# Where and when the tokens of attention and MLP are turned in the fused third stage

## What is computed

```python
x = x + _L0_attn_ref(_layernorm(x), Wkqv, bkqv, Wp, bp)      # causal attention, 16 heads
x = x + _L0_ffn_ref(_layernorm(x), gate_w, ...)              # 16 experts, top 4, and a shared one
x = x + _L1_attn_ref(_layernorm(x), wq, wk, wv, wo)          # 16 heads of 8, hyperbolic distance
x = x + _L1_ffn_ref(_layernorm(x), w1, b1, w2, b2)           # relu(x @ w1 + b1) @ w2 + b2
```

## Time and profile before

| what | us |
|---|---|
| median of 3 runs | 2449.32 |
| lowest, highest | 2448.59, 2451.76 |
| profiled execution, its time | 2456.33 |
| profiled execution, its span | 2454.2 |
| third stage's loop in it, end of the first `dve_ratio` of body 0 to that of body 31 | 1343.48 to 2372.66 |

### The profile page before, as it was taken

The page is one execution under the profiler, slowest core; times in us unless marked ns, Lnnn a source line. Parts: engine busy times, 40 slices in busy tenths (PEclk is TensorE's granted clock), DMA queues, the critical chain, the costliest instruction groups (busy, mean ns, idle before and its releaser), DMA issues. The chain is left out here.

```text
span 2454.2 us, 50808 instructions
## 1 busy us (share of the span) xinstructions
PE 2089.9 (85%) x15438; PEld 1566.8 (64%) x15438; DVE 1956.8 (80%) x5939; ACT 1767.4 (72%) x3085; POOL 1627.2 (66%) x1866
## 2 busy tenths in 40 slices
PE   4999999999999996999997677777777778777876
PEld 4677777777777775888885445555555555555554
DVE  4677776776777774778775899999999999999992
ACT  2666666666666762444432799999999999999996
POOL 2776676766666750000001899999999999999993
PEclk7999999999999996999997579888888988889888
DMA  5000000000000003353450466776666777666674
GB/s 142 1 2 2 2 1 2 2 1 2 1 2 1 2 2 70 86 119 76 96 114 10 93 127 130 139 138 128 124 119 127 141 141 134 119 129 124 129 142 80
DMA packets 81388, 184.24 MB, mean 75 GB/s; under 512 B 9479, under 2 KB 31530, under 8 KB 81195
## 3 DMA queue, kind: packets, MB, share of 16 engines
q0 software_dynamic: 36864, 134.23, 29.1%
q1 hardware_dynamic: 36010, 43.38, 7.9%
q10 hardware_dynamic: 8320, 4.19, 0.7%
HBM read 42.85 MB, written 4.72 MB: 19 GB/s over the span
## 5 line engine op out<-in xcount | busy, mean ns | idle before, releaser
L1557 POOL TENSOR_TENSOR spare<-spare,u 128x1024 f32<-128x1024 f32 x192 | 456.2, 2376 | 16.0
L542 ACT ACTIVATE prob<-s_ps,nmax 128x128 f32<-128x128 f32 (+1 forms) x1024 | 364.4, 432 | 132.2 <-DVE nmax L599 132.2
L599 DVE CUSTOM_DVE_ANT_0 s_ps<-s_ps,mask 128x128 f32<-128x128 f32 (+1 forms) x1024 | 340.7, 385 | 100.7 <-issue 76.4
L1633 DVE TENSOR_SCALAR u<-d_ps 128x1024 f32<-128x1024 f32 x256 | 312.1, 1219 | 48.7 <-PE i_ps L1374 48.1
L579 POOL TENSOR_TENSOR g_lo<-g_all,g_hi 128x512 fp32r<-128x512 f32 x256 | 329.1, 1286 | 21.4
L1637 DVE SCALAR_TENSOR_TENSOR u<-i_ps,u 128x1024 f32<-128x1024 f32 x256 | 313.5, 1225 | 13.2 <-DVE u L1633 0.5
L1374 PE MATMUL d_ps<-rowsT 28*128 28x256 f32 x1024 | 144.7, 357 | 149.5 <-DVE u L1637 145.9
L534 ACT COPY g_all<-g_ps 128x512 f32<-128x512 f32 x256 | 151.5, 592 | 162.6 <-PE g_ps L63 161.5
L1514 ACT ACTIVATE u<-u 128x1024 f32<-128x1024 f32 x256 | 257.0, 1056 | 1.7 <-DMA u<-spare 1.6
L1517 ACT ACTIVATE u<-u 128x1024 f32<-128x1024 f32 x256 | 255.7, 1051 | 0.0
L1374 PEld LDWEIGHTS d_ps<-rowsT 28*128 28x128 f32 x1024 | 92.4, 208 | 246.3 <-issue 241.7
(11 more groups left out here) (275 smaller groups left out, 5795.2 us busy)
## 6 DMA issues: line engine op xcount, KB each, us to landing
u<-spare POOLq DMA_DIRECT2D x256, 512.0 KB, 12.2
w_all<-w_rows SPq DMA_DIRECT2D x128, 256.0 KB, 5.9
x<-L_attn_x ACTq DMA_DIRECT2D x8, 512.0 KB, 13.9
y<-x SPq DMA_DIRECT2D x32, 128.0 KB, 10.0
wkqv<-L_attn_Wkqv SPq DMA_DIRECT2D x4, 528.0 KB, 8.9
gate_rows<-L_ffn_gate_proj SPq DMA_DIRECT2D x1, 512.0 KB, 14.4
up_rows<-L_ffn_up_proj SPq DMA_DIRECT2D x1, 512.0 KB, 11.1
down_cols<-L_ffn_down_proj SPq DMA_DIRECT2D x1, 512.0 KB, 13.0
```

What stands on the lines that cost most here:

```text
L542: last = nc.scalar.activation(prob[:, kind, at, :].rearrange("p c n -> p (c n)"), s_ps[kind][:, at.start * P:at.stop * P], ACT.Exp, bias=n ...
L599: last = nc.vector.tensor_tensor_reduce(out=scores, in0=scores, in1=keep.mask[:, N - width:N], scale=-1.0, scalar=3.4e38, op0=ALU.add, op1 ...
L1557: nc.gpsimd.tensor_tensor(extra, extra, pair, ALU.mult).then_inc(prod_done, 1)
L1633: nc.vector.tensor_scalar(u[:, slot(i, p), :], d_ps[:, :], 0.0, None, ALU.max).then_inc(dist_done, 1)
```

## The change

The two pairs of transposes leave step 0 of PE's body and the bank `misc`. They go to the end of step 7 of the body before, behind the projection and the last transposes of rows, into `o_ps` (all 512 columns), whose content DVE has copied out by then (`o_copied`). ACT's one copy reads `o_ps` instead of `misc`. `pe_turn_x4` thereby takes batch b-3 in body b in place of b-4 in body b, so it stands one body earlier in the list than before, by a few instructions. The round of `pe_keep_busy` in step 7, which wrote into `o_ps`, is removed. Since `pe_y` writes `o_ps` too, PE now waits in step 0 for ACT's copy (`xT_done`, in the last body `late_xT4_done`) before `pe_y`. The wait for `res_done` moves from the transposes to `pe_qkv`. In the prologue PE waits for ACT's copy of w1 (`w1_folded`) and turns batch 1 before the loop; the wait for `w1_folded` in `pe_hidden` is dropped.

```diff
--- before.py
+++ after.py
@@ -1251,7 +1251,7 @@
     VALUES_AT = (2, 3, 4, 5)
     BACK_AT, ATTN_AT, PROJECT_AT = 4, 6, 7
     HIDDEN_AT = (1, 3)
-    BUSY_AHEAD, BUSY_BEHIND = {5: 1}, {4: 4, 7: 1}
+    BUSY_AHEAD, BUSY_BEHIND = {5: 1}, {4: 4}
     HW = WB // 2
     NORM_BEHIND, NORM4_BEHIND = 2, 5
     with ExitStack() as stack:
@@ -1336,15 +1336,15 @@
 
         def pe_turn_x(pe, b):
             pe.wait_ge(xh_done, (b + 1) * TB)
-            after(pe, res_done, b - 3)
-            after(pe, hi_done, b * TB)
-            after(pe, qkv_taken, b * TB)
+            after(pe, xT_done, b)
             for j in range(TB):
-                last = nc.tensor.transpose(misc[:, j * P:(j + 1) * P], xh[:, j, :], keep.ident)
+                last = nc.tensor.transpose(o_ps[:, j * P:(j + 1) * P], xh[:, j, :], keep.ident)
             last.then_inc(xh_turned, 1)
 
         def pe_qkv(pe, b, j):
             pe.wait_ge(xT_done, b + 1)
+            if j == 0:
+                after(pe, res_done, b - 3)
             after(pe, hi_done, b * TB + j)
             after(pe, qkv_taken, b * TB + j)
             nc.tensor.matmul(misc[:, 0:3 * P], xTs[:, 0, j * P:(j + 1) * P], keep.qkvoT[:, 0:3, :], start=True,
@@ -1423,6 +1423,7 @@
 
         def pe_fold_w1(pe):
             pe.wait_ge(weights_in, 16 * 5)
+            pe.wait_ge(xT_done, 1)
             nc.tensor.matmul(o_ps[:, :], zsum[:, :], w1_rows[:, :], start=True, stop=False)
             nc.tensor.matmul(o_ps[:, :], last_row[:, :], b1_row[:, :], start=False, stop=True).then_inc(w1_ready, 1)
 
@@ -1433,8 +1434,6 @@
             last.then_inc(x4_turned, 1)
 
         def pe_hidden(pe, b, half, rows_read):
-            if half == 0:
-                pe.wait_ge(w1_folded, 1)
             pe.wait_ge(rowsT_done[half], rows_read)
             after(pe, relu_done, 2 * b - 1 + half)
             for n in range(HW):
@@ -1465,14 +1464,14 @@
         def act_xT(act, b):
             act.wait_ge(xh_turned, b + 1)
             after(act, qkv_ready, b * TB)
-            nc.scalar.copy(xTs[:, 0, :], misc[:, 0:N]).then_inc(xT_done, 1)
+            nc.scalar.copy(xTs[:, 0, :], o_ps[:, 0:N]).then_inc(xT_done, 1)
 
         def act_both_xT(act, b, b4):
             act.wait_ge(xh_turned, b + 1)
             act.wait_ge(x4_turned, b4 + 1)
             after(act, qkv_ready, b * TB)
             after(act, h_ready, 2 * b4)
-            nc.scalar.copy(xTs[:, :, :].rearrange("p s n -> p (s n)"), misc[:, :]).then_inc(xT_done, 1)
+            nc.scalar.copy(xTs[:, :, :].rearrange("p s n -> p (s n)"), o_ps[:, :]).then_inc(xT_done, 1)
 
         def act_hi(act, b, j):
             act.wait_ge(qkv_ready, b * TB + j + 1)
@@ -1712,18 +1711,14 @@
                     pe_turn_rows(pe, 0, p)
                 pe_pairs(pe, 0, 0, 0)
                 pe_fold_w1(pe)
+                pe.wait_ge(w1_folded, 1)
+                pe_turn_x(pe, 1)
 
                 def body(b, i, one_before, two_before, three_before, four_before, five_before, one_after, two_after):
                     for p in range(HP):
                         following = next_pair(b, p, one_after)
                         if following:
                             pe_pairs(pe, *following, i if p + 1 < HP else (i + 1) % TURN)
-                        if one_after and p == 0:
-                            pe_turn_x(pe, b + 1)
-                        if four_before and p == 0:
-                            if not one_after:
-                                pe.wait_ge(res_done, b - 2)
-                            pe_turn_x4(pe, b - 4, (i - 4) % TURN, misc, N)
                         if one_after and p == 1:
                             pe_qkv(pe, b + 1, 0)
                         for r in {0: (5, 6), 1: (7,)}.get(p, ()):
@@ -1748,15 +1743,22 @@
                         if one_after:
                             for r in {6: (2,), 7: (4,)}.get(p, ()):
                                 pe_turn_rows(pe, b + 1, r)
+                        if p == HP - 1 and one_after:
+                            if one_before:
+                                pe.wait_ge(o_copied, 2 * b)
+                            if two_after:
+                                pe_turn_x(pe, b + 2)
+                            if three_before:
+                                pe_turn_x4(pe, b - 3, i, o_ps, N)
                         if one_before:
-                            if p == HP - 1:
-                                pe.wait_ge(o_copied, 2 * b)
                             pe_keep_busy(BUSY_BEHIND.get(p, 0))
+                        if p == 0 and one_after:
+                            pe.wait_ge(xT_done, b + 2)
+                        if p == 0 and not one_after:
+                            pe.wait_ge(late_xT4_done, 1)
                         if five_before and p == 0:
                             pe_y(pe, b - 5, 2 * (b - 1))
                         if four_before and p == HIDDEN_AT[0]:
-                            if not one_after:
-                                pe.wait_ge(late_xT4_done, 1)
                             pe_hidden(pe, b - 4, 0, (b + 1) * (HP // 2))
                 over_batches(pe, body)
 
@@ -1828,7 +1830,7 @@
                         else:
                             act_xT(act, b + 1)
                     elif four_before:
-                        act_late_xT4(act, b - 4, misc[:, N:2 * N])
+                        act_late_xT4(act, b - 4, o_ps[:, N:2 * N])
                     for p in range(0, HP, 2):
                         if one_before:
                             weights(b - 1, (i - 1) % TURN, p)
```

## The result

The changed kernel takes 2472.97 us (median of 4 runs, 2472.11 to 2473.70), the kernel before beside it 2449.18; the ratio is 1.0097, 95% interval 1.0084 to 1.0109. The prediction said 2451.0 with a range of 2437 to 2464: the kernel is 22 us slower than that and lies above the range, on the side of rival (a). The profiled execution took 2473.7 us (span 2471.7), 17.4 more than that of before. The medians differ by 23.8, because the profiled execution of before lies 7.2 us above its median and that of after only 0.7; these 6.4 us are in no trace. 15.4 of the 17.4 us are in the loop.

What follows compares the result with a forecast made beforehand. No engine's share decides; the exchange between DVE and PE sets a body's length in its first 14 us. Prologue +1.5 and the clean, in-between and late boundaries sum to +1.7 us: 2449.3 + 1.7 = 2451.0, range 2437 to 2464.

Steps and rivals of the forecast that it cites:

- rival (a): Clock falls more often, right behind clean boundaries: +8 to +13 us, around 2461; chance 0.34 together with another rival.
- ACT is not the bound: ACT's copy loses up to 14.0 us of idle, which comes back at the second ReLU; taken as 0.
- The good boundary, +0.5: Full-clock boundary: pe_y waits for ACT's copy until about +2.75, DVE goes on at 4.94 instead of 4.43: +0.5 us.
- the 0.28 us of waiting for POOL: Clean boundary: MLP's transposes wait for pool_norm4, DVE stalls 0.28 us at dve_distances of pair 1, contained in the +0.5.
- The late boundary, -0.5: Half-clock boundary: pe_y starts earlier, dve_y's stall of 0.40 us vanishes; with -0.1 from the transposes, -0.5 us.
- the -0.1: Late boundary: four transposes take 0.9 us where PE now gets to pe_pairs 0.99 later: -0.1 us.
- 7 x 0.5 - 2 x 0.5 + 9 x 0.3 - 10 x 0.5: Loop's terms: clean boundaries, two clean with half clock behind them, those in between, and late ones, counted in the old trace.
- Its sign, a mean clock below 0.86: Sign of more clock falls: the loop's mean granted clock below 0.86, with many a pe_y at half clock.
- The prologue, +1.5: Loop's first pe_pairs waits for ACT's copy of w1, ending 2.10 us behind the first boundary: +1.5, bounds 0 and 2.5.

Runs made afterwards that it cites:

- hold3_n4_after: Changed kernel with hold3's fillers (none ahead of pair 1), one filler round ahead of the moved transposes, and pool_norm4 two steps earlier: 2448.16 us, 1.0029.
- hold3: Both kernels with idle matmuls in pe_pairs (two ahead of pair 6) and three filler rounds in step 4; changed one none at pair 1: 2427.08 before, 2461.00 changed.
- hold2_after: Changed kernel with idle matmuls in pe_pairs of all seven stretches, four ahead of pair 6, and three filler rounds ahead of step 4's values: 2463.09 us, 1.0088.
- fillback: Changed kernel with one filler round put back in step 7, ahead of the moved transposes: 2475.94 us, 1.0101.
- hold_before: Kernel before with idle matmuls in pe_pairs, pair 6 left out, and three filler rounds ahead of step 4's values: 2475.54 us, 1.0113.
- midhold_before: Kernel before with only the three filler rounds ahead of step 4's values added: 2446.25 us, 0.9990.
- hold3_before: Kernel before with idle matmuls in pe_pairs of all seven stretches, two ahead of pair 6, and three filler rounds ahead of step 4's values: 2427.08 us, 0.9928.
- delay_before: Kernel before with one added DVE copy of 128 x 256 in step 0 into a tile that nothing reads: 2450.28 us, 1.0026.
- hold3_fill_after: Changed kernel with hold3's fillers (none ahead of pair 1) and one filler round back ahead of the moved transposes: 2454.90 us, 1.0053.
- nofill: Kernel before with only the filler round at the end of step 7 removed: 2463.07 us, 1.0053.
- edge_hold2_after: hold2_after with the products of pair 1 issued ahead of the jump of PE's loop: 2480.98 us, 1.0182.

## Why the prediction was wrong

- **ACT is not the bound**: right. 11.9 us less waiting at the copy, no gain at the end; part shows again at the second ReLU.
- **The good boundary, +0.5**: right in size, 0.44 at a steady clock; `pe_y` was forecast at +2.75, DVE behind it at +4.94, and at 1674.61 they came at +2.61 and +4.90. The step that the 0.28 us of waiting for POOL are contained in this holds too: hold3_n4_after takes them away and gains nothing in a body.
- **The turn of the loop**: not seen. 0.27 us in every third body, 2 us. I put no term for it into the sum; in the old order PE's wait for DVE hides it.
- **The late boundary, -0.5**: right in size where the clock comes back as in before. Body 7 takes 33.28 and has no `dve_y` stall, against 33.9 before; pair 1 waits 0.82 us there as before, so the -0.1 in it did not come.
- **The step that failed is the count of the boundaries.** 7 x 0.5 - 2 x 0.5 + 9 x 0.3 - 10 x 0.5 multiplied each price by the number of such boundaries in before, which puts at nothing what the change does to the clock's falls. The change itself sets these numbers. Of the 26 bodies from the sixth on, after has 8 in which PE waits for ACT's copy; 5 late ones that gain as forecast; 7 late ones whose half clock goes on through `pe_y`; in all 10 with a stall at `dve_y` of over 0.5 us; and 11 bodies of the loop with a stall of over 1.2 us at pair 6, for which the sum had no term. These show in the waits: 8.4 us more at pair 6, 3.5 at pair 1, 2.8 at `dve_y`. Where the sum had +1.7 us, the profiled loop has +15.4.
- **Rival (a)** had the right kind of cause and was too small: +8 to +13 for falls behind good boundaries. Bodies 9, 11 and 12 are of its kind (`dve_y` waits 0.89, 1.63 and 1.30 us). It did not have the falls in the middle of the body, where filler turns from cover into obstacle. Its sign, a mean clock below 0.86, came only as 0.85 (321 us of the loop at half clock against 288): the mean moved little, the places did.
- **The prologue, +1.5**: wrong. Body 0 became 0.8 us shorter (32.07 against 32.86), and its first products waited 0.57 us instead of 1.36, a stall that before already had and the sum did not count. ACT's copy of w1 ended 0.19 us behind the first boundary, not 2.10:

```profile
1342.07 0.59 ACT L1526 COPY w<-o_ps 128x512 f32<-128x512 f32 x1 [5.19 <-PE o_ps L1428]
```

The loop's start lies between 1330 and 1343 in these runs, whatever the kernel, so the stage ahead of the loop and the 3.1 us behind it can't be told from chance.

What is shown: at a steady clock the new order costs 0.44 us a body, 0.70 at the loop's turn, and the wait for POOL is no part of it; in the old order the filler's removal alone costs 13.5 us, with the half clock at other places. What is argued from rows: that the 0.44 us are the wait for ACT's copy. What is not shown: why the falls settle at just these places, and how the 23.8 us divide. The 13.3 us of the wait and the 13.5 of the filler must not be added up: after has the wait in 8 bodies and not in 26, and putting the round back into after gave nothing. No run brought the changed kernel back to the time of before without the fillers of hold3.

## What to carry to other kernels

A copy that joins two paths in one buffer makes the later user of the buffer wait for it: price that wait first, for an iteration at full clock. It depends on the slack of the reader: 0.44 us a body in hold3, where ACT's copy starts at +1.91, none in hold2_after, where it starts at +1.25. Don't multiply a price by the number of good and bad iterations of the old trace when the change touches what makes them good or bad; hold the clock steady in both versions and compare there. Filler belongs where the engine waits anyway and nothing due is queued behind: a round takes 1.06 us instead of 0.60 when the clock is down, and in fillback it raised the wait of pair 1 at late boundaries from 0.82 to 1.67 us.

## What the runs showed of the hardware

- A higher mean granted clock with more time: 0.95 and 2475.5 us (hold_before), 0.86 and 2449 (before), 0.91 and 2446 (midhold_before), 0.99 and 2427 (hold3_before). In these kernels the place of the half-clock stretches counts for more than their total, 113 us of the loop in hold_before against 288 in before.
- Bodies lock: 34.13 us in each body of hold_before from body 6 on, and a cycle of three bodies of 98.99 us in before and in delay_before, though the latter has more work in each.
- Behind PE's jump back in its loop pair 1's products start 0.3 to 0.4 us later where the moved transposes end shortly before (hold2_after, hold3_fill_after), and not at all where PE idles for DVE there (nofill). A stop of 8.12 us in such a body occurred once (edge_hold2_after); that the jump caused it is not shown.
